# Fused four-stage block on Trainium2: low parts of two of three tiles of h by subtraction on VectorE in the last stage

## The reference

```python
xq = nvfp4_qdq(x2[:, up_reorder_index], SEL_UP)
wg = nvfp4_qdq(w_gate[:, up_reorder_index], SEL_UP)
wu = nvfp4_qdq(w_up[:, up_reorder_index], SEL_UP)
h = jax.nn.silu(xq @ wg.T) * (xq @ wu.T)          # 1024 x 1376
hq = nvfp4_qdq(h[:, down_reorder_index], SEL_DOWN)
wd = nvfp4_qdq(w_down[:, down_reorder_index], SEL_DOWN)
out = hq @ wd.T * mlp_output_scale
out = out + x2 @ lr_A @ lr_B
```

## Time and profile before

| | before |
|---|---|
| median of 3 runs | 858.9 us |
| lowest and highest | 858.37 and 859.61 us |
| the profiled execution | 862.48 us |
| its span, first to last instruction | 861.2 us |
| PE busy | 736.4 us, 86% |
| DVE busy | 579.2 us, 67% |
| ACT busy | 430.6 us, 50% |
| mean granted TensorE clock | 0.921 of full speed |

### The profile page before, as it was taken

The page is one execution under the profiler, slowest core; times in us unless marked ns, Lnnn a source line. Parts: engine busy times, 40 slices in busy tenths (PEclk is TensorE's granted clock), DMA queues, the critical chain, the costliest instruction groups (busy, mean ns, idle before and its releaser), DMA issues.

```text
span 861.2 us, 11244 instructions
## 1 busy us (share of the span) xinstructions
PE 736.4 (86%) x4112; PEld 545.7 (63%) x4112; DVE 579.2 (67%) x1107; ACT 430.6 (50%) x549; POOL 189.9 (22%) x176
## 2 busy tenths in 40 slices
PE   1797754988999988999999898586799799959998
PEld 1564421656777666766766677474578688957886
DVE  4899977563686867889788586754644333567873
ACT  3756665555876847797877111252243121224452
POOL 0223000021253433355354463032011000000000
PEclk9999855889999999999999999887599899997999
DMA  7644668775375647576663110111111010200001
GB/s 275 208 138 169 214 197 285 242 233 181 125 231 183 199 169 241 174 249 214 225 198 118 58 38 21 51 49 54 45 33 41 21 46 25 67 17 12 25 25 37
DMA packets 56039, 110.55 MB, mean 128 GB/s; under 512 B 9888, under 2 KB 20800, under 8 KB 55984
## 3 DMA queue, kind: packets, MB, share of 16 engines
q1 hardware_dynamic: 42560, 78.43, 28.1%
q10 hardware_dynamic: 9040, 17.30, 6.0%
q0 software_dynamic: 4384, 14.09, 5.6%
HBM read 91.65 MB, written 18.15 MB: 128 GB/s over the span
## 4 chain that ended last, share of the span: by engine, by line
PE 57%; DVE 23%; DMA 7%; ACT 6%; issue 6%; SPq 1%; ACTq 0%; DVEq 0%
PE bank L1110 15%; PE bank L1111 14%; PE bank L1112 14%; PE bank L1213 3%; DVE hot L1747 2%; ACT hot L1501 2%; PE bank L1394 2%; DVE bank L1773 2%; PE bank L1226 1%; DMA wide_buf<-in_down_flat 1%; DMA codes<-c 1%; DVE gm L1789 1%; DVE x L1870 1%; DVE x L1711 1%; PE bank L1243 1%
## 5 line engine op out<-in xcount | busy, mean ns | idle before, releaser
L1501 ACT ACTIVATE hot<-rep,levels 128x2048 f16<-128x2048 f16 x96 | 193.6, 2057 | 19.6 <-ACT c L1464 10.3
L1110 PE MATMUL bank<-zt_h,w_h 128*128 128x512 f32 (+1 forms) x232 | 96.4, 415 | 4.5 <-DVE x L1870 2.5
L1111 PE MATMUL bank<-zt_l,w_h 128*128 128x512 f32 (+1 forms) x232 | 93.3, 402 | 0.0
L1112 PE MATMUL bank<-zt_h,w_l 128*128 128x512 f32 (+1 forms) x232 | 93.2, 402 | 0.0
L1213 PE MATMUL bank<-hot,diag 128*32 128x512 f16 x1160 | 82.3, 412 | 7.7 <-DVE hot L1747 4.9
L1110 PE MATMUL bank<-w_h,xq_h 128*128 128x512 f32 (+1 forms) x192 | 74.7, 389 | 4.6 <-DVE w_l L1888 4.6
L1111 PE MATMUL bank<-w_l,xq_h 128*128 128x512 f32 (+1 forms) x192 | 72.6, 378 | 0.0
L1112 PE MATMUL bank<-w_h,xq_l 128*128 128x512 f32 (+1 forms) x192 | 72.6, 378 | 0.0
L2013 POOL TENSOR_TENSOR q_a<-q_a,q_m 128x384 f32<-128x384 f32 (+3 forms) x34 | 37.0, 1089 | 112.8 <-DVE q_m L1641 112.7
L1985 DVE TENSOR_TENSOR hid<-hid,bank 128x512 f32<-128x512 f32 (+1 forms) x24 | 15.1, 628 | 67.3 <-PE bank L1112 43.6
L1213 PEld LDWEIGHTS bank<-hot,diag 128*32 128x32 f16 x1160 | 26.7, 100 | 53.1 <-issue 26.7
(11 more groups left out here) (219 smaller groups left out, 1676.1 us busy)
## 6 DMA issues: line engine op xcount, KB each, us to landing
rep<-codes SPq DMA_DIRECT2D x58, 512.0 KB, 4.8
codes<-c SPq DMA_DIRECT2D x29, 256.0 KB, 4.6
raw<-in_codes_gu_t ACTq DMA_DIRECT2D x14, 512.0 KB, 5.6
sc<-in_scales_gu_t SPq DMA_DIRECT2D x56, 128.0 KB, 3.9
raw<-in_codes_attn_t ACTq DMA_DIRECT2D x8, 512.0 KB, 4.4
raw<-in_codes_down_t ACTq DMA_DIRECT2D x7, 512.0 KB, 5.7
sc<-in_scales_down_t SPq DMA_DIRECT2D x28, 128.0 KB, 3.2
wide_buf<-in_gate_flat SPq DMA_DIRECT2D x5, 512.0 KB, 4.2
```

The source lines that it names most:

```text
L1110: PE.matmul(psum, lh, rh, start=first, stop=False, **kw)
L1111: PE.matmul(psum, lh, rl, start=False, stop=False, **kw)
L1112: return PE.matmul(psum, ll, rh, start=False, stop=last, **kw)
L1501: S.activation(hots[plan.slot[hot_ring(t), (t, m)]][:], codes_in_place(t), ACT.Relu, bias=bias, scale=slope).then_inc(sem("ramp_act"), 1)
```

## The change

For items A and B of h, `low` is replaced by a new step, `less`, in the same place of the list. It has no PE part and no ACT part: DVE waits for `take` of the item and subtracts the high part from the bank, writing the low part. `hprod` of A and B waits for DVE in place of ACT, and the bank of the transposes is freed by DVE. Item C, and the items of x in the earlier stage that uses the same generator, keep `low`.

```diff
@@ -750,6 +750,12 @@
     greatest_of_all("x")
     p.add("scale", "x", 0, NT)
 
+    def less(item):
+
+        return item[0] == "h" and item[2] < len(CHUNKS) - 1
+
+    p.less = less
+
     def turned_tiles(items):
 
         staged = turned = split = None
@@ -763,10 +769,10 @@
                 p.take("q_tmp", 2, item, ("dve", "qturn", *item))
                 p.take("q_out", 2, item, ("pe", "qturn", *item))
             if turned:
-                p.add("low", *turned)
+                p.add("less" if less(turned) else "low", *turned)
             if staged:
                 p.add("qturn", *staged)
-                turn4(staged, ("act", "low", *staged))
+                turn4(staged, ("dve", "less", *staged) if less(staged) else ("act", "low", *staged))
                 p.add("take", *staged)
                 if staged[0] == "h":
                     p.take("hq", 4, staged, ("pe", "hprod", *staged))
@@ -1405,7 +1411,7 @@
             elif kind == "hprod":
                 _, n, c = key
                 (ph, pl), bank = hq[plan.slot["hq", key]], main4(("d", n))
-                pe.wait_ge(*done("act", "low", *key))
+                pe.wait_ge(*(done("dve", "less", *key) if plan.less(key) else done("act", "low", *key)))
                 pe.wait_ge(*done("dve", "drow", c, KD - 1))
                 if c == 0:
                     for m in vacant("main4", ("d", n)):
@@ -1976,6 +1982,12 @@
                     dve.wait_ge(*m)
                 V.tensor_tensor(blocks_of(q_out[plan.slot["q_out", key]], nq), blocks_of(ua, nq),
                                 spread_of(c, P, nq), ALU.mult).then_inc(sem("qturn_dve"), 1)
+            elif kind == "less":
+                dve.wait_ge(*done("act", "take", *key))
+                for lo, hi, nr in split_runs(item_tiles(key)):
+                    last = V.tensor_tensor(quant_place(key, 1, nr, lo, hi), turned_view(turn(key), nr, lo, hi),
+                                           quant_place(key, 0, nr, lo, hi), ALU.subtract)
+                last.then_inc(sem("less_dve"), 1)
             elif kind == "hfin":
                 c, n = key
                 f0, w = CHUNKS[c]
```

## The result

| | before | after |
|---|---|---|
| median of the runs made side by side | 859.91 us (6 runs) | 872.56 us (6 runs) |
| ratio, with its 95% interval | | 1.0135 (1.0101 to 1.017) |
| repeated later beside 17 runs of before | 861.37 us | 871.78 us, ratio 1.0112 (1.0077 to 1.0147) |
| span of the profiled execution | 861.2 us | 870.7 us |
| last stage, first `round` to the end | 89.37 us | 99.25 us |

The change makes the kernel slower by 1.1 to 1.35%. The length of the last stage, read from the profile, doesn't have that spread.

What follows compares the result with a forecast made beforehand. PE was taken to bound the last stage. Start +2.82, middle row tiles +6.05 and last row tile +1.00 gave +9.9 us on 858.9, so 868.8 us, range 864.5 to 873.5.

Steps and rivals of the forecast that it cites:

- What bounds the kernel: Last stage: PE runs without a gap at 9.65 us a row tile; DVE runs ahead and waits for it.
- What goes costs nothing and gives nothing: 16 `minus` matmuls leave PE, 0.23 us each, 0.46 less a row tile; 16 ACT copies count as nothing.
- Load fits, wait does not: DVE's load becomes 8.8 us a row tile, under PE's 9.19; its wait in the queue decides.
- Loop from A to B: A's transposes to B's, through PE, ACT and DVE: 4.09 us against 3.30 of PE's own work; PE waits 0.79.
- Loop from B to C: B's transposes to C's, through PE, ACT and DVE: 3.20 us against 2.53 of PE's own work; PE waits 0.67.
- C to A: C's transposes to the next A's: no closed loop; DVE's way 3.25 us, PE's own 3.36 is longer.
- Row tiles together: Transposes of the second A to those of the last: 6 x 10.65 = 63.90 us instead of 57.85, +6.05.
- The start: First row tile, empty pipeline, lower clock level: first product at 784.13 us and not 781.31, +2.82 us.
- Rival 1: DVE's waits don't reach PE: row tiles take PE's 9.19 us, 3.7 us less, 855.2 us; chance 5%.
- Rival 2: PE's pauses lower the clock for half of each row tile: 1.2 us more for 7 tiles, some 877 us; 6%.
- Rival 3: Waits eat what the 16 matmuls give back: row tile within 0.2 us of 9.65, about 859 us; chance 3%.
- The weighed rule on DVE: Subtraction to line 1971: 0.60 us taken from the trace; by the skill page some 0.72, each loop 0.12 longer.

Runs made afterwards that it cites:

- the run with nothing removed: Kernel before, all its matmuls and copies kept, plus DVE's wait for ACT's copy and a same-size scratch subtraction: ratio 1.0132, stage 99.28 us.
- work only: Kernel before plus a same-size scratch subtraction on DVE at the new step's place, waiting for nothing: ratio 0.9992, stage +0.34 us.
- wait only: Kernel before plus DVE's wait for ACT's copy at the new step's place, no subtraction: ratio 1.004, stage +2.75 us.
- the fastest kernel: Changed kernel with the subtraction behind the three finishing operations and `fin` one iteration later: 857.29 us, ratio to before 0.9956, stage 85.23 us.
- before with `fin` later: Kernel before with `fin` one iteration later and nothing else: ratio 0.9992, stage -0.98 us, row tile 9.48 us.
- subtraction behind: Changed kernel with each subtraction moved behind the three operations finishing the next item: median 858.6 us, ratio to before 0.9971, stage -1.86 us.
- A alone: Changed kernel with the new step for item A only, B keeping `low`: stage +5.27 us against before, single execution.
- B alone: Changed kernel with the new step for item B only, A keeping `low`: stage +4.86 us against before, single execution.

## Why the prediction was right, point by point

The forecast was 868.8 us within 864.5 to 873.5, the measured median 872.56, and +9.9 us was forecast against the kernel before. The medians are 12.65 us apart in the first comparison and 10.4 in the second. Inside the stage the growth is 9.88 us. That this agrees with 9.9 to 0.02 us is luck: the start came out 0.33 us above its forecast and the row tiles 0.33 below. So is part of the place in the range: added to the 859.91 us of the runs side by side, the forecast would have been 869.8. The 2.8 us between 12.65 and 9.88 lie outside the last stage or in the spread of the runs; the interval of the first ratio is 1.01% to 1.7%, or 8.7 to 14.6 us, so the prediction's 1.7 us as what a measurement can tell was too small.

- **What bounds the kernel.** PE at 9.65 us a row tile: right, but for the 0.17 us of waiting with `fin`, which I took for PE's own time. The prediction read `fin`'s wait (3.41 us, at the start of the stage; in the steady row tiles it is 1.95) as a sign that DVE was ahead, and it was a tie. PE's own time with the change's work is 9.03 us, not the 9.19 of the text.
- **What goes costs nothing and gives nothing.** Shown by the run with nothing removed: 99.28 against 99.25 us.
- **Load fits, wait does not.** Shown by the runs with work only (+0.34 us) and with wait only (row tile +0.04 us).
- **Loop from A to B**: 4.09 us forecast, 4.06 measured. Its terms: transposes to copy 0.69 forecast and 799.91 - 799.27 = 0.64 measured; copy to subtraction 0.61 and 0.62; subtraction to line 1977 0.60 and 0.61; the three operations 2.13 and 2.13; to PE 0.06 and 0.06. The one term that was off is the first: when PE had waited, the group takes 0.66 and the copy comes after 0.69 (803.33 to 804.02), and at A it had not waited. PE's idle column shows 0.65 and 0.47 us where the prediction has 0.79 and 0.67. The waits are nevertheless as large as forecast: against PE's own 3.24 and 2.53 us in the fastest kernel the distances are 0.82 and 0.68 us longer. The column counts the last product ahead of the pause as busy for 0.40 us, while products follow each other 0.23 us apart.
- **Loop from B to C**: 3.20 forecast, 3.21 measured. The prediction let DVE's other work in this window (`round`, once two more operations) vanish behind the wait of 1.36 us. It did in each row tile, and where the two operations stood it was close: the B subtraction without a bracket. **C to A**: 3.36 forecast, 3.32 measured.
- **Row tiles together**: 6 x 10.65 - 57.85 = 6.05 us forecast; 852.25 - 788.68 = 63.57 us measured, so 5.72. Last row tile +1.00 forecast, 7.26 - 6.29 = 0.97 measured.
- **The start**: +2.82 us forecast, 13.64 - 10.49 = 3.15 measured. The two loops gave 4.57 + 3.67 - 3.01 - 2.38 = 2.85, as forecast. The other 0.30 us is C to A, 5.40 for 5.10 us. Of it 0.05 lies ahead of the first product, which came 0.55 us after C's transposes and not 0.50. The rest is the step "I take it to rise as late after it as before". The granted clock of 780 to 790 us, 0.76 before and 0.61 now, puts the rise at 784.8 and 787.8 us; that is 3.5 us after the first product before and, with the first product at 783.83, 4.0 us after it now.
- **Rival 1** (load decides, faster) needed loops below PE's own time. They become that when the subtraction stands behind the three operations, but that alone gives -1.86 us; its time comes out only with `fin` later too, and a little more (-4.20 us for its 3.7).
- **Rival 2** (the clock gives way) fell: granted clock 1.00 in each 10 us from 790 to 860 us, with pauses of 0.65 and 0.47 us in each row tile. By the page TensorE: Matmul & The Clock Gate of the Trainium skill, section A second HAM failure mode: psum-queue depth-cycling, which tells of such a swing with short pauses between groups of matmuls, it was the likelier case. This trace does not agree: these pauses did not bring the clock down.
- **Rival 3** (no change) needed a row tile within 0.2 us of 9.65; it is 10.59.
- **The weighed rule on DVE.** The page VectorE: DVE Perf Modes of the Trainium skill, section The DRAIN you can't avoid, reports the same time for a chain of eight copies with a semaphore after each and with one after the last. The prediction worked out from it that the 0.60 us would be 0.72. But the same section also says that a next operation which is not held starts earlier, and that part fits these rows. That a semaphore costs nothing does not: in the changed kernel the unbound pair starts 801.14 - 800.53 = 0.61 us apart and the bound pair, whose second operation waits for the first, 801.86 - 801.14 = 0.72.

## What to carry to other kernels

Before moving an operation to an engine that seems to have room, look at what stands behind it in that engine's queue, and who waits for that. If the operation waits for something that itself depends on the queue's own earlier output, add up the loop once around and compare it with the bounding engine's own time per round. Here the place of one step in the queue turned the same work from +9.9 us into -1.9 us in the stage, and a second wait (`fin`), moved behind urgent work, gave the rest of the 4.2 us. The sizes hold for this kernel.

## What I had not expected

**Kernels with the same first distances had the clock rise at the same point.** C to A in the first row tile, which holds 12 products and the rise of the clock, took 5.10, 5.11 and 5.11 us in the three kernels whose first two distances are 3.01 and 2.35 to 2.38 us (before, before with `fin` later, subtraction behind), 5.13 and 5.16 in the two profiles of the best kernel; 5.40, 5.41 and 5.42 in the three profiles with 4.57 and 3.67; but 5.94 with wait only, 4.81 with work only, 4.34 with A alone and 6.11 with B alone, each of these four from one profile. It does not simply grow with the delay of the first products. The first tile with B alone was at the lower level to its end:

```profile
776.00:789.10 13.10, 9.08 (x26) 6.60 (x27) 11.43 (x21) 3.83 (x9) 0.00 (x0) 0.50 0.00 0
```

What sets the moment is left open; no run here varied it by itself. For sizes it means that a change at the start of this stage can gain 0.8 us or lose 1.0 (4.34 and 6.11 against 5.10 us) with the clock.

**A small wait can hide in a busy engine.** PE was busy for all of 800 to 840 us in the kernel before and in the one with `fin` later, yet a row tile differs by 0.17 us. The time that a group of transposes takes, 0.66 or 0.60 us, shows it where the idle column does not.
